# Decoder on one core: the feed-forward's weights loaded and summed in the stage before it, and rounded one at a time

## What is computed

```python
def _weight_quant(w):
    scale = 1.0 / jnp.clip(jnp.mean(jnp.abs(w)), 1e-05)
    return jnp.clip(jnp.round(w * scale), -1.0, 1.0) / scale
def _act_quant(x):
    scale = 127.0 / jnp.clip(jnp.max(jnp.abs(x), axis=-1, keepdims=True), 1e-05)
    return jnp.clip(jnp.round(x * scale), -128.0, 127.0) / scale
def _bitlinear(x, w):
    return jnp.einsum('bsi,oi->bso', _act_quant(x), _weight_quant(w))
gate = jax.nn.silu(_bitlinear(x, w_gate))
x = _layernorm(x + _bitlinear(gate * _bitlinear(x, w_up), w_down))
```

## Time and profile before

| | us |
|---|---|
| median of 3 runs | 3981.87 |
| lowest and highest | 3979.12 and 3982.95 |
| the profiled execution, its own time | 3985.28 |
| span of the profiled execution | 3983.5 |
| busy in the span: PE, DVE, ACT, POOL | 3356.9, 3184.3, 2746.4, 2621.1 |
| feed-forward stage: its first instruction | 3633.39 after the start |
| feed-forward stage: first `ff_h` | 3669.92 |

### The profile page before, as it was taken

One profiled execution on the slowest core, in us unless ns is written; L12 is line 12 of the kernel. 1 busy time (PEld: TensorE's weight loads), 2 busy tenths in 40 slices (PEclk: granted clock), 3 DMA queues, 4 the chain that ended last, 5 costly groups with the idle time before them and its releaser, 6 DMA issues. The chain is left out here.

```text
span 3983.5 us, 73736 instructions
## 1 busy us (share of the span) xinstructions
PE 3356.9 (84%) x22592; PEld 2487.1 (62%) x22592; DVE 3184.3 (80%) x5336; ACT 2746.4 (69%) x5012; POOL 2621.1 (66%) x2794
## 2 busy tenths in 40 slices
PE   8996999979953688888898988889888779995887
PEld 5664666667531467676776767667677657773555
DVE  5665888845394799899898989988898668896998
ACT  2223777744474788788887888888788557774776
POOL 1223767630093698899898989989899646662555
PEclk9998999979976899999999999999999989997999
DMA  2111221151122111111111111111111122222111
GB/s 61 56 53 51 51 48 47 48 105 36 42 50 63 42 49 55 53 49 52 47 55 52 55 53 49 52 47 57 49 49 49 40 52 55 55 54 75 54 58 38
DMA packets 284832, 209.68 MB, mean 53 GB/s; under 512 B 131208, under 2 KB 249544, under 8 KB 284504
## 3 DMA queue, kind: packets, MB, share of 16 engines
q1 hardware_dynamic: 284504, 205.72, 18.6%
HBM read 149.18 MB, written 51.41 MB: 50 GB/s over the span
## 5 line engine op out<-in xcount | busy, mean ns | idle before, releaser
L2806 POOL TENSOR_TENSOR ma_ch<-ma_h,ma_crep 128x512 f32<-128x512 f32 x1024 | 1376.4, 1363 | 180.9 <-DVE ma_h L2908 171.4
L2908 DVE TENSOR_TENSOR_SCAN ma_h<-ma_a,ma_pbu 128x512 f32<-128x512 f32 x1024 | 1215.5, 1207 | 198.3 <-PE ma_pbu L2494 133.4
L2494 PE MATMUL ma_pbu<-ma_ident,ma_bu 128*128 128x128 f32 x4096 | 658.3, 284 | 223.2 <-DVE ma_h L2908 182.6
L2494 PEld LDWEIGHTS ma_pbu<-ma_ident,ma_bu 128*128 128x128 f32 x4096 | 475.0, 144 | 463.7 <-DVE ma_h L2908 359.6
L2696 ACT ACTIVATE ma_a<-ma_dt,ma_A 128x510 f32<-128x510 f32 x1024 | 652.8, 716 | 1.7 <-issue 1.7
L2503 PE MATMUL ma_py<-ma_ident,ma_ch 128*128 128x128 f32 x4096 | 624.7, 278 | 0.8 <-POOL ma_ch L2806 0.8
L2503 PEld LDWEIGHTS ma_py<-ma_ident,ma_ch 128*128 128x128 f32 x4096 | 494.7, 145 | 11.4 <-issue 10.2
L2687 ACT ACTIVATE ma_bu<-ma_uT,ma_b_t 128x512 f32<-128x512 f32 x736 | 478.5, 718 | 27.1 <-PE ma_pbu L2494 25.4
L881 POOL TENSOR_TENSOR xa_prob<-xa_e,xa_rec_head 128x616 f32<-128x616 f32 x128 | 153.1, 1216 | 120.5 <-DVE xa_rec_head L971 120.4
L1513 POOL TENSOR_TENSOR xa_prob<-xa_e,xa_rec_head 128x616 f32<-128x616 f32 x128 | 155.5, 1216 | 92.4 <-DVE xa_rec_head L1606 91.5
L337 POOL TENSOR_TENSOR la_veps<-la_mv,la_eps 128x2 f32<-128x2 f32 x32 | 6.2, 195 | 250.4 <-DVE la_mv L370 250.4
(11 more groups left out here) (353 smaller groups left out, 8020.5 us busy)
## 6 DMA issues: line engine op xcount, KB each, us to landing
ma_crep<-ma_ct_dram SPq DMA_DIRECT2D x256, 256.0 KB, 3.2
xa_x<-act SPq DMA_DIRECT2D x64, 256.0 KB, 2.9
act<-xa_y SPq DMA_DIRECT2D x64, 256.0 KB, 2.1
la_x<-in_x SPq DMA_DIRECT2D x32, 256.0 KB, 2.7
act<-la_y SPq DMA_DIRECT2D x32, 256.0 KB, 2.2
ea_x<-act SPq DMA_DIRECT2D x32, 256.0 KB, 11.4
act<-ea_x SPq DMA_DIRECT2D x32, 256.0 KB, 4.0
ma_x<-act SPq DMA_DIRECT2D x16, 512.0 KB, 4.6
```

The costliest lines, as they stand in the source:

```text
L2494: last = pe.transpose(pbu[c % 2][:, t * P:(t + 1) * P], bu[:, s % 2, t, c * P:(c + 1) * P], ident[:, :])
L2806: pool.tensor_tensor(ch[:, s % 2, c], h[:, s % 2, c], crep[:, s % 4, :], ALU.mult).then_inc(multiplied, 1)
L2908: dve.tensor_tensor_scan(out=h[:, s % 2, c, :], data0=a[:, s % 2, c, :], data1=pbu[c % 2][:, :], initial=0.0, op0=ALU.mult, op1=ALU.add).t ...
```

## The change

The weights' float32 tiles, the identity and the tile of sums move out of `bit_ffn` into a stage `fw` around the last two stages. SP issues their loads in 13 pieces (the identity, eight halves of rows of gate and up, four pairs of down's rows; 256 KB each but the first) in the cross attention's batches 4 to 16, one per batch. VectorE sums the three weights at the cross attention's end: one in the last batch before `residual(30)`, one between `moments(30)` and `residual(31)`, one behind `moments(31)`. In the feed-forward each weight is scaled, clipped and cast by itself, with the leading slots put between them on each engine; PE waits for a weight (`w_ready`) only where it first uses it; ScalarE applies Silu once to a spare element ahead of everything.

```diff
+class FeedForwardWeights:
+    def __init__(self, st, wgu_d, wd_d, ident_d):
...
+        self.pieces = [(self.ident[:, :], ident_d)]
+        for m in range(2):
+            up = wgu_d[m].rearrange("(c p) i -> p c i", p=P)
+            self.pieces += [(self.wgu_f[:, m, c, i:i + 512], up[:, c, i:i + 512]) for c in range(C) for i in range(0, I, 512)]
+        self.pieces += [(self.wd_f[:, c:c + 2, :], down[:, c:c + 2, :]) for c in range(0, I // P, 2)]
@@ cross attention, SP, per batch n, behind load_x
+                if ffn_weights is not None and 4 <= n < 4 + len(ffn_weights.pieces):
+                    sp.dma_start(*ffn_weights.pieces[n - 4]).then_inc(f_loaded, 16)
@@ cross attention, VectorE
+                if nxt is None:
+                    weight_sums(0)
                 if before is not None:
                     residual(*before)
...
+            def weight_sums(m):
+                if ffn_weights is not None:
+                    dve.wait_ge(f_loaded, 16 * len(ffn_weights.pieces))
+                    dve.tensor_reduce(ffn_weights.wsum[:, m:m + 1], ffn_weights.whole(m), AX.X, ALU.add, apply_absolute_value=True)
...
             moments(last_batch[0], last_batch[1] - 1)
+            weight_sums(1)
             residual(*last_batch)
             moments(*last_batch)
+            weight_sums(2)
@@ feed-forward
+        def lead(slot, *slots):
+            for n in slots:
+                slot(n % 2, *[divmod(n + d, BT) if n + d >= 0 else None for d in AROUND])
@@ SP
-            for dst, src in ((ident[:, :], ident_d), (wgu_f[:, 0], wgu_d[0].rearrange("(c p) i -> p c i", p=P)),
-                             (wgu_f[:, 1], wgu_d[1].rearrange("(c p) i -> p c i", p=P)),
-                             (wd_f[:, :, :], wd_d.rearrange("(c p) f -> p c f", p=P))):
-                sp.dma_start(dst, src).then_inc(w_loaded, 16)
@@ PE (project waits w_ready m + 1 and down waits w_ready 3, at the first tile only)
-            pe.wait_ge(wsum_ready, 1)
+            pe.wait_ge(ones_ready, 1)
             pe.matmul(pd[:, 0:3], ones[:, :], wsum[:, :], start=True, stop=True).then_inc(wtotal_made, 1)
-            pe.wait_ge(setup_done, 1)
+            lead(slot, -4, -3, -2)
+            lead(slot, -1)
@@ ScalarE
+            def weight(m):
+                w, q = weights[m]
                 act.wait_ge(w_clipped, m + 1)
+                act.activation(q, w, ACT.Copy, bias=-ROUND).then_inc(w_ready, 1)
+            act.activation(warm[:, :], wsum[:, 0:1], ACT.Silu)
             act.sem_inc(g_ready, 1)
+            weight(0)
+            lead(slot, -4, -3, -2)
+            weight(1)
+            lead(slot, -1)
+            weight(2)
@@ GpSimd
-            pool.wait_ge(setup_done, 1)
+            pool.wait_ge(wmean_ready, 1)
+            lead(slot, -4, -3, -2, -1)
@@ VectorE
+            def weight(m):
+                w, _ = weights[m]
+                link(dve.tensor_scalar(w, w, wscale[:, m:m + 1], ROUND, ALU.mult, ALU.add))
+                dve.tensor_scalar(w, w, ROUND - 1.0, ROUND + 1.0, ALU.max, ALU.min).then_inc(w_clipped, 1)
...
+            weight(0)
+            lead(slot, -4, -3)
+            weight(1)
+            lead(slot, -2, -1)
+            weight(2)
             tiles(dve, slot, link)
```

More of the change, by code:

```diff
@@ L126, in split_in_three, with whole @@
                                     scalar=pick[:, k:k + 1], in1=rest[:, :], op0=ALU.mult, op1=ALU.add))
+class FeedForwardWeights:
+    def __init__(self, st, wgu_d, wd_d, ident_d):
+        self.I = I = wd_d.shape[0]
+        self.ident = st.sb("ident", [P, P])
+        self.wgu_f = st.sb("wgu_f", [P, 2, C, I])
+        self.wd_f = st.sb("wd_f", [P, I // P, D])
+        self.wsum = st.sb("wsum", [P, 3])
+        down = wd_d.rearrange("(c p) f -> p c f", p=P)
+        self.pieces = [(self.ident[:, :], ident_d)]
[3 more added lines that the diff above has]
+        self.pieces += [(self.wd_f[:, c:c + 2, :], down[:, c:c + 2, :]) for c in range(0, I // P, 2)]
+    def whole(self, m):
+        w = self.wd_f[:, :, :] if m == 2 else self.wgu_f[:, m]
+        return w.rearrange("p c i -> p (c i)")
 def linear_attention(nc, x_in, x_out, wqT, bq, wkvT, bkv, woT, bo, ident_d, blocks_d):
@@ L1127, in cross_attention_in_halves @@
         mask_loaded = [sem(f"mask_loaded{q}") for q in range(2)]
+        f_loaded = sem("f_loaded")
         v_copied, kheads_ready = sem("v_copied"), sem("kheads_ready")
@@ L3034, in bit_ffn @@
         sb, ps, sem = st.sb, st.ps, st.sem
-        ident = sb("ident", [P, P])
         ones = sb("ones", [P, P])
-        wgu_f = sb("wgu_f", [P, 2, C, I])
-        wd_f = sb("wd_f", [P, IC, D])
         wgu = sb("wgu", [P, 2, C, I], bf16)
         wd = sb("wd", [P, IC, D], bf16)
-        wsum = sb("wsum", [P, 3])
         wmean = sb("wmean", [P, 3])
         wscale = sb("wscale", [P, 3])
+        warm = sb("warm", [P, 1])
         eps = sb("eps", [P, 1])
@@ L3133, in _, with is_first @@
         def _(pe):
+            def is_first(tile):
+                return type(tile[0]) is int and tile == (0, 0)
             def project(tile, m, out, done):
                 k = tile[1]
+                if is_first(tile):
+                    pe.wait_ge(w_ready, m + 1)
                 for half in range(2):
@@ L3145, in down @@
                 pe.wait_ge(res_added, count(tile))
+                if is_first(tile):
+                    pe.wait_ge(w_ready, 3)
                 for c in range(IC):
@@ L3321, in _ @@
             link = Chain(dve, chain, 6 * BT)
[L3322 to L3326, removed]
+            def weight(m):
+                w, _ = weights[m]
+                link(dve.tensor_scalar(w, w, wscale[:, m:m + 1], ROUND, ALU.mult, ALU.add))
+                dve.tensor_scalar(w, w, ROUND - 1.0, ROUND + 1.0, ALU.max, ALU.min).then_inc(w_clipped, 1)
+            dve.memset(ones[:, :], 1.0).then_inc(ones_ready, 1)
             dve.wait_ge(wtotal_made, 1)
             link(dve.tensor_scalar(wmean[:, :], pd[:, 0:3], 1.0 / (I * D), FLOOR, ALU.mult, ALU.max))
+            dve.sem_inc(wmean_ready, 1)
             link(dve.reciprocal(wscale[:, :], wmean[:, :]))
[L3330 to L3334, removed]
             dve.sem_inc(h_ready, 1)
@@ L3361, in decoder @@
     if STAGES > 4:
[L3362 to L3366, removed]
+        with Stage(nc, "fw") as fw:
+            ffn_weights = FeedForwardWeights(fw, a["L1_ffn_wguT"], a["L1_ffn_wdT"], a["ident"])
+            cross_attention_in_halves(nc, "xa1", acts[4], acts[5], a["ctx"], a["L1_xattn_WqT"], a["L1_xattn_WkvT"], a["L1_xattn_WoT"],
+                                      a["L1_xattn_bo"], a["ident"], a["head_columns"], bq_d=a["L1_xattn_bq"],
+                                      bk_d=a["L1_xattn_bk"], bv_d=a["L1_xattn_bv"], ffn_weights=ffn_weights)
+            if STAGES > 5:
+                bit_ffn(nc, acts[5], acts[6], ffn_weights)
 def kernel(**inputs):
```

15 lines of the change are left out of this document (6 added, 9 removed).

## The result

The changed kernel takes 3956.89 us (median of 4 runs, 3953.90 to 3959.88); the kernel before, run beside it, takes 3982.05 (4 runs, 3979.12 to 3982.95). The ratio on record is 0.9942, with a 95% interval of 0.9930 to 0.9955; the two medians alone give 0.9937, inside it. The profiled execution of the changed kernel took 3955.68 us, its span is 3953.9 and its mean granted clock 0.949; those of before are 3985.28, 3983.5 and 0.946. The forecast was 3958.4, with a range of 3955.0 to 3963.5.

What follows compares the result with a forecast made beforehand. Preparation alone filled the feed-forward's first 36.5 us, then VectorE set the pace. Terms -24.0 (start) + 0 (tail) + 0 (issues) + 0.2 (traffic) + 0.3 (barrier) = -23.5 took the median 3981.87 to 3958.4 us, range 3955.0 to 3963.5.

Steps and rivals of the forecast that it cites:

- Stage start, -24.0: Feed-forward's start to first `ff_h`: falls from 36.5 to 12.5 us as load and sums leave it, a gain of 24.0.
- The tokens' room of a microsecond: Feed-forward's start: tokens needed at +3.93 us, least load time 2.9, so one microsecond to spare.
- Tail, 0: Cross attention's end: three sums of 2.28 us fit VectorE's waits and the time behind the last statistics, costed at nothing.
- SP's issues, 0 within 0 to 6.6: SP's queue in cross attention: thirteen issues, 6.6 us of queue, fit SP's waits for PE; taken as 0, at most 6.6.
- the other case: Rival that SP's queue was full after all: 13 x 0.51 us on the path, ending at 3965.0; chance 0.08.
- The further room of 2.0 in front of PE: Cross attention: v's spread lands 2.0 us before PE takes it, slack beyond SP's own wait.
- Traffic, +0.2: Cross attention: the pieces' bytes delay transfers behind them, taken as 0.2 us in all; at worst 28 before room.
- a twelfth of another transfer's delay: Basis of the 0.2 us: one piece is 1/12 of the 3 MB of weights ahead of the slow `ff_x` loads.
- The rival by which bytes hold the spread's issues: Cross attention: pieces' bytes make v late in thirteen batches, costing 21 or 49 us; chance of a loss over 8 us 0.03.
- End barrier, +0.3: Kernel's end: the weights' own stage adds one clearing and barrier, taken as 0.3 us, bounds 0 to 0.7.
- The rival with the late rise: Feed-forward's first tiles: TensorE's clock rises three microseconds later, costing about 2 us, ending at 3960.4; chance 0.12.
- The baseline: Whole kernel: the same -23.5 us takes the profiled 3985.28 to 3961.8 and the median 3981.87 to 3958.4.

## Why the prediction was right

- **Stage start, -24.0.** Measured -23.74. The branch that ends last is the one named: up weight's cast, up matmuls, `ff_h`. Against the prediction's times from the stage's start the clip of the first weight ended at +4.31 (forecast +3.93), the tokens' scaling began at +6.16 (+5.8), the second cast ended at +10.65 (+10.45), the gate activation at +12.01 (+11.7), the up matmuls at +12.65 (+12.4), and `ff_h` began at +12.79 (+12.5). The whole difference stands at the front: total, mean and reciprocal were put at 1.1 and took 1.5, since four increments of semaphores now lie between them. An increment that shows as 0.02 us holds VectorE's queue for 0.1. The two branches end 0.64 apart, where 0.8 was forecast. The tokens' room of a microsecond was right: the first loads landed after 2.8, and VectorE came to them without a wait. The sizes of the parts are shown by the three kernels that undo them (6.1, 11.1, 6.5).
- **Tail, 0.** Right. The kernel without the sums in the tail has a cross attention of the same length (445.5), and with all sums last the tail pays 1.4, so the cover is real and has an end.
- **SP's issues, 0 within 0 to 6.6.** Right, and closer than a chance of 0.08 for the other case says: the room is 0.3 a batch by the queue of the kernel with three more issues. SP's waits fell to 0.36 in the mean, where 0.3 was forecast. The further room of 2.0 in front of PE is borne out: the kernel with one more issue lost 0.9 of a slip of 2.6.
- **Traffic, +0.2.** Neither confirmed nor refuted. The stage is 0.25 longer. It takes 444.95 and 445.26 in the two profiles whose cross attention has no pieces, and 445.4 to 445.8 in the six that have one a batch and no more load; so a few tenths are likely, but in the longest of the six 0.3 stand ahead of the first piece. The 0.2 itself came from a twelfth of another transfer's delay, and no run shows that term. The rival by which bytes hold the spread's issues is excluded: large and tiny loads cost the same, and 3.2 MB in one batch did not stretch them. What made the token loads slow in the earlier trace rows is there again in the kernel that only changes the order, with 1 MB in each transfer ahead of them; thirteen transfers of 256 KB or less did not do it. Whether it is the size of one transfer or the form of its lines was not separated. The place that the prediction quoted from the Trainium skill (DMA: Bandwidth & Descriptors, Queues, rings and completion order), that a ring is taken in order, agrees with the traces, and so does what the prediction made of it: behind large loads the spread's first transfers land late (the tenth step at 3.6 to 4.1 us, and at 5.3 behind all pieces, in place of 2.0), its last ones do not.
- **End barrier, +0.3.** Measured 0.3 from TensorE's last group to the end.
- **The clock.** The rival with the late rise did not come. The clock rose at 3641.2, at `ff_h` itself, where before it rose 3.8 us behind it (3673.7 against 3669.92). In the seven profiles whose feed-forward code is the changed kernel's the rise lies between 0.6 us ahead of the first `ff_h` and 2.0 behind it. The latest, with all sums last, still took 296.0 from first to last `ff_h`, so a rise 2 us late cost nothing there; a later one was not seen with this code. Without the early Silu the clock fell once more at 3649.3, and first to last `ff_h` took 296.75, 0.7 more. What was not foreseen is the other end: in before's profiled execution a fall in the last microseconds cost 1.56.
- **The baseline.** The forecast took the median as moving with the profiled execution. For that execution it said 3961.8, and it took 3955.68, 6.1 less, most of it the 5.2 of drift ahead of both stages. The medians moved by 25.2 us, 23.1 by the ratio on record (its interval is 18 to 28 us), and the prediction was 23.5; the trace's own sum for the change is 23.74 (stage start) - 0.25 (cross attention) - 0.35 (first to last `ff_h`) - 0.3 (barrier) = 22.8. So each large term is right by itself, but that the median came within 1.5 us of 3958.4 is partly luck: the interval of the ratio is 5 us to either side. The 0.35 stood in no term of the forecast. Of it 0.37 comes at one place: VectorE's maximum of the fifth `ff_h` stands 0.52 us behind it in the changed kernel and 0.15 before. The step from the fifth `ff_h` to the sixth is 5.5 instead of 5.16 in every profile of the new code; why was not found.

## What to carry to other kernels

A stage's start that only loads and prepares weights is worth its whole length when no work covers it, and its parts can be priced one by one: follow both branches to the first real product, since the removal of a step is worth only the distance to the branch that ends next (0.5 for a table load of 1.28). Before work is put into a queue that looks idle, count what its period holds against the loop's period: here the one piece a batch fit with 0.3 us to spare, a second issue beside it cost 0.9 in all, and three turned more than half of the gain into waits (13.6 us), whatever their size. Compare two profiles stage by stage before a difference of spans is given to the change: here the 29.6 us held 5.2 of drift and 1.6 of a clock that fell in one execution.

## What the runs showed of the hardware that was not expected

- After one wait of 4.76 us in a busy loop TensorE's granted clock was at its low level for the next 4.9 us, and the stage lost 1.7 to 1.9 more than the wait. At the kernel's end it fell in or up to 1.4 us behind a wait of 2.25 in four profiles and held in nine. Twelve of the thirteen run the changed kernel's code at this place.
- GpSimd's `ff_fgu`, 128x4 elements, took 1.07 and 1.16 us in the first tokens, where it takes 0.20 elsewhere. In both cases VectorE was scaling a weight from SBUF to SBUF (3633.67 to 3634.94, and 3637.11 to 3638.38), and the small operation ended 0.05 us behind it. During the sums in the cross attention's tail GpSimd's small operations kept their 0.20. The Trainium skill (SBUF — State Buffer, SBUF: two separate sides) has it that VectorE and GpSimd share a pair of ports, and that a VectorE instruction in a 2-port mode, or a GpSimd instruction, whichever starts first, holds the pair for its whole length while the other waits; the trace agrees with the wait, but that the scaling is in such a mode is not shown. Nothing waited for it here.
- An increment of a semaphore that stands by itself between two VectorE instructions costs about 0.1 us of its queue: from mean to first scaling it is 0.82 with four of them, and 0.40 without, before and again in the kernel that scales ahead (3623.26 to 3623.66).
- A DMA's place in SP's queue and its transfers are two prices. Behind large loads a spread's first transfers landed up to 3.3 us later, while its last one, issued ten microseconds on, landed as ever; only the issues' time reached PE.
